# Causal depthwise filters of a two-layer decoder: from four 128x32 column tiles to sixteen 32x32 tiles, with a new order of all steps

## What is computed

```python
v_direct = silu(causal_conv4(h @ Wv))               # 128 channels = 4 heads x 32
delta_out = delta_rule_chunkwise(q, k, v_direct, beta)      # chunks of 32: a triangular solve in each
paths = [fir(v_direct, w) for w in (fir_w3, fir_w7, fir_w15, fir_w31)] + [delta_out]
# fir: causal, depthwise: y[ch, t] = sum_j w[ch, j] * v[ch, t - j]
mix = softmax(router(h, *paths) / tau)              # per token, head and path
o = sum(mix_i * path_i) * (1 - p) + v_direct * p    # then a norm per head, Wo, residual, layer norm
```

## Time and profile before

| | us |
|---|---|
| median of 3 runs (lowest, highest) | 1003.74 (1002.26, 1004.86) |
| span of the profiled execution | 1004.1 |
| PE busy | 932.3 |
| DVE busy | 742.6 |
| ACT busy | 650.3 |
| POOL busy | 334.5 |

### The profile page before, as it was taken

One profiled execution on the slowest core, in us unless ns is written; L12 is line 12 of the kernel. 1 busy time (PEld: TensorE's weight loads), 2 busy tenths in 40 slices (PEclk: granted clock), 3 DMA queues, 4 the chain that ended last, 5 costly groups with the idle time before them and its releaser, 6 DMA issues.

```text
span 1004.1 us, 22014 instructions
## 1 busy us (share of the span) xinstructions
PE 932.3 (93%) x7958; PEld 593.9 (59%) x7958; DVE 742.6 (74%) x2882; ACT 650.3 (65%) x1474; POOL 334.5 (33%) x720
## 2 busy tenths in 40 slices
PE   6988899999986989999999999999977899999996
...
DVE  3556789899899986866374797869999996665514
...
PEclk7999999999987799999999999999986999999998
...
GB/s 308 175 2 1 1 1 52 2 83 14 95 128 75 43 70 17 44 22 12 1 12 1 11 11 1 53 60 94 90 97 76 57 21 22 2 11 1 12 1 32
DMA packets 77692, 45.44 MB, mean 45 GB/s; under 512 B 53008, under 2 KB 68880, under 8 KB 77328
## 3 DMA queue, kind: packets, MB, share of 16 engines
...
## 4 chain that ended last, share of the span: by engine, by line
PE 57%; DVE 27%; ACT 8%; POOL 4%; issue 3%; DMA 0%; SPq 0%; POOLq 0%; ACTq 0%; DVEq 0%
PE psum L1101 7%; DVE pool L1588 5%; DVE sol_t L1593 5%; PE psum L558 5%; PE psum L1091 4%; PE psum L859 4%; PE psum L833 3%; PE psum L831 3%; PE psum L994 3%; DVE pool L1531 3%; PE psum L920 3%; PE psum L1085 2%; PE psum L1087 2%; ACT pool L1823 2%; PE psum L567 2%
## 5 line engine op out<-in xcount | busy, mean ns | idle before, releaser
L1809 ACT ACTIVATE pool<-psum 128x512 f32<-128x512 f32 x144 | 84.0, 595 | 64.4 <-PE psum L558 22.4
L2185 POOL TENSOR_SCALAR small<-small 128x4 f32<-128x4 f32 x88 | 22.2, 252 | 283.6 <-DVE small L1173 281.4
L1823 ACT ACTIVATE pool<-pool,small 128x128 f32<-128x128 f32 x224 | 91.5, 486 | 27.3 <-POOL small L2190 27.1
L558 PE MATMUL psum<-sb_const,pool 128*128 128x128 f32 x672 | 100.9, 283 | 6.4 <-ACT pool L1823 2.9
L920 PE MATMUL psum<-pool,firw 128*32 128x512 f32 (+7 forms) x960 | 103.2, 571 | 0.0
L558 PEld LDWEIGHTS psum<-sb_const,pool 128*128 128x128 f32 x672 | 79.3, 145 | 37.9 <-issue 22.3
L2188 POOL TENSOR_TENSOR small<-small,minus_half 128x4 f32<-128x4 f32 x88 | 92.2, 1048 | 7.3
L994 PE MATMUL psum<-pool,sb_l1a 128*128 128x512 f32 x192 | 88.6, 612 | 0.0
L1101 PEld LDWEIGHTS psum<-sb_l1f,pool 128*128 128x128 f32 x640 | 77.2, 192 | 11.3 <-issue 9.5
L1101 PE MATMUL psum<-sb_l1f,pool 128*128 128x128 f32 x640 | 82.8, 278 | 0.0
L1404 DVE TENSOR_TENSOR pool<-pool,psum 128x512 f32<-128x512 f32 x80 | 52.4, 682 | 37.8 <-ACT pool L2095 16.2
...
## 6 DMA issues: line engine op xcount, KB each, us to landing
...
```

Source lines behind the costliest of these rows:

```text
L558: m = e.transpose(f.ap[:, part(b)], src[:, part(b)], ident)
L1809: e.activation(slot(g, i), f.ap, ACT.Copy).then_inc(f.emptied, 1)
L1823: m = e.activation(dst[:, part(b)], src[:, part(b)], ACT.Identity, bias=v["nm"][:, b:b + 1], scale=v["r"][:, b:b + 1])
```

## The change

What it does, part by part:
- **b_fir** is one step with four banks. The contraction of 32 rows is now 4 shifts x 8 channels, and the 32 outputs of a tile are 4 filters x 8 channels. Row tile r is a head, column tile c a quarter of its channels. All filters are padded with zeros to eight tap groups: 8 x 16 = 128 products a group of 32x32, bank r for row tile r.
- **b_sh** writes v to DRAM in four DMAs, which reorder the channels so that a read of stride 4 finds shift s on partitions s, s+4, ...; the four reads go to partitions of stride 4.
- **b_ez** is one multiply on POOL of the first three columns of each of 16 blocks by a column of zeros and ones; it also waits for `s_b2`.
- **b_mx, b_ac, b_w, b_lt**: paths now lie as (head, batch, quarter, filter, channel), so the mixing weights are laid out by head and spread first (`spread`), and the sum over filters is taken inside the tile: low and high halves (POOL for slots 3 and 4, DVE for 5 and 6), then neighbours.
- **Setup**: `s_w` (new) sorts the taps on PE in 16 small products and copies them; `s_b2` clears `firw` and fills it in 16 small multiplies. `l1a` is loaded by 18 DMAs instead of one, since the router's rows for slots 3 to 6 are reordered.
- **ORDER** is new as a whole.

```diff
+NKG = 8
-    firw, itau = sb("firw", [P, nfg * 4, CH]), sb("inverse_tau", [P, NH])
+    firw, itau = sb("firw", [P, NKG, 4, 32]), sb("inverse_tau", [P, NH])
-for _name in ("b_kk", "b_at"):
+for _name in ("b_kk", "b_at", "b_fir"):
...
 def b_sh(g, k):
+            by_row = kept.rearrange("(r u c) m -> r c u m", r=4, c=4)
-            e.dma_start(kept, slot(g, 5)).then_inc(sem(f"v_out{a}"), 16)
-            o.wait_ge(sem(f"v_out{a}"), 16 * (g // NA + 1))
+            for r in range(4):
+                e.dma_start(by_row[r], slot(g, 5)[32 * r:32 * r + 32]).then_inc(sem(f"v_out{a}"), 16)
+            o.wait_ge(sem(f"v_out{a}"), 64 * (g // NA + 1))
             for s in range(4):
-                e.dma_start(vsh[32 * s:32 * s + 32, :, s:],
-                            kept.rearrange("(c p) m -> p c m", c=4)[:, :, 0:GT - s]).then_inc(sem(f"shifted{a}"), 16)
+                e.dma_start(vsh[s:P:4, :, s:],
+                            kept.rearrange("(u c) m -> u c m", c=4)[:, :, 0:GT - s]).then_inc(sem(f"shifted{a}"), 16)
...
-        for p_ in ("l1a", "l0f"):
-            load(p_)
+        load("l1a", 0, rw1 + 256)
+        load("l1a", rw1 + 5 * 256)
+        for c in range(4):
+            for f in range(4):
...
+                e.dma_start(dst[32 * c + 8 * f:32 * c + 8 * f + 8], src).then_inc(sem("ld_l1a"), 16)
+        load("l0f")
...
 def b_fir(g, k):      # PE
-            f = begin("b_fir", g, "s", k)
+            heads_f = [begin("b_fir", g, f"h{r}") for r in range(4)]
...
+            for kg in range(NKG):
+                for r in range(4):
+                    r_ = slice(32 * r, 32 * r + 32)
+                    for c in range(4):
+                        m = e.matmul(b4(heads_f[r].ap)[32 * c:32 * c + 32, :, 4 * kg:], firw[r_, kg, c, :],
+                                     vsh[r_, c, :, 0:P - 4 * kg], start=kg == 0, stop=kg == NKG - 1)
+                    if kg == NKG - 1:
+                        m.then_inc(heads_f[r].filled, 1)
...
 def b_mx(g, k):       # DVE
-            e.tensor_tensor(hd(p), hd(f.ap), rep(w3[:, :, k], DH), ALU.mult).then_inc(f.emptied, 1)
-            if k >= 2:
+            e.tensor_tensor(slot(g, 3 + k).rearrange("p (q f u) -> p q f u", f=4, u=8),
+                            f.ap.rearrange("p (q f u) -> p q f u", f=4, u=8), share, ALU.mult).then_inc(f.emptied, 1)
+            if k == 3:
...
+                e.tensor_tensor(low, low, high, ALU.add).then_inc(*o.link())
...
 def b_fir(g, k):      # ACT
-            evacuate("b_fir", g, 3 + k, k)
+            for r in range(4):
+                f = full("b_fir", g, f"h{r}")
+                e.activation(slot(g, 3 + r), f.ap, ACT.Copy).then_inc(f.emptied, 1)
...
 def b_ez(g, k):       # POOL
-            for s in range(1, 4):
-                settle()
-                e.memset(vsh[32 * s:32 * s + 32, :, :, 0:s], 0.0).then_inc(*mark("edge_zeroed", 3 * g + s))
+            o.wait_ge(made, MADE["s_b2"])
...
+            e.tensor_tensor(cells, cells, shift_col[:, 0:3].unsqueeze(1).to_broadcast([P, NP, 3]), ALU.mult).then_inc(
+                *mark("edge_zeroed", g + 1))
```

More of the change, by code:

```diff
@@ L48 @@
[L48 to L82, removed]
@@ L103 @@
-b_x.32-41/4 b_vT/5 b_x.42-44/4 b_fir.1/5 b_q2/6 f_na/7 b_fir.2-3/5 b_kk/5 b_fir.0/6 b_x.45-52/4 b_ag/5 b_x.53-58/4
-b_vT/6 b_x.59/4 b_ss/6 b_x.60-61/4 b_xo/4 b_tr/7 b_q/7 b_k/7 b_qs/7 b_v/7 b_vs/7 b_sol/5 b_x.0-1/5 b_qn/6 b_x.2-3/5
-b_gg/6 b_x.4-6/5 b_ks/7 b_k2/7 b_fir.1/6 b_x.7/5 b_fir.2/6 b_x.8-20/5 b_fir.3/6 b_rs/4 b_xt/4 b_x.21/5 b_rl/4 b_u.0/4
-b_x.22/5 b_sh/7 b_kk/6 b_x.23-26/5 b_ag/6 b_x.27-31/5 b_p.0/4 b_q2/7 b_ss/7 b_x.32-34/5 b_u.1/4 b_x.35-39/5 b_ez/7
-b_x.40-43/5 b_qn/7 b_x.44-47/5 b_gg/7 b_x.48-51/5 b_fir.0/7 b_vT/7 b_p.1/4 b_x.52-53/5 b_fir.1/7 b_sol/6 b_x.0/6
@@ new lines @@
+b_ez/2 b_x.61/0 b_x.8-9/1 b_tr/3 b_qn/2 b_x.10/1 b_xo/0 b_gg/2 b_rs/0 b_x.11-14/1 b_v/3 b_xt/0 b_k/3 b_x.15-16/1 b_q/3
+b_x.17-18/1 b_vs/3 b_ks/3 b_x.19/1 b_k2/3 b_rl/0 b_x.20-24/1 b_qs/3 b_fir/2 b_x.25-26/1 b_sh/3 b_x.27-31/1 b_q2/3 b_ez/3
+b_kk/2 b_x.32/1 b_u.0/0 b_x.33-38/1 b_ag/2 b_ss/3 b_x.39/1 b_qn/3 b_x.40-41/1 b_p.0/0 b_x.42-48/1 b_vT/3 b_sol/2
+b_x.49/1 b_u.1/0 b_x.50-51/1 b_gg/3 b_x.52-54/1 b_x.0/2 b_x.55/1 b_x.1-4/2 b_fir/3 b_x.5/2 b_x.56/1 b_x.6-7/2 b_x.57/1
+b_x.8/2 b_x.58/1 b_x.9/2 b_x.59/1 b_x.10/2 b_x.60/1 b_x.11-12/2 b_x.61/1 b_x.13-14/2 b_xo/1 b_x.15-22/2 b_rs/1
```

263 lines of the change are left out of this document (174 added, 89 removed).

## The result

| | before | after |
|---|---|---|
| median of the runs shown | 1004.22 us | 1010.33 us (1008.83 to 1012.08) |
| ratio, 95% interval | | 1.0059 (1.004 to 1.0079) |
| span of the profiled execution | 1004.1 us | 1007.0 us |
| mean granted clock of TensorE | 0.959 | 0.955 |
| filter line: PE busy | 103.2 us | 69.3 us |

The account below looks back on a forecast made before the run. Bound by PE, with two patches bound by DVE. Shortening the two stretches with filters gave -38 us, banks +3, other terms zero: -35 from the profiled 1004.1 us, so 969 us; range 947 to 998.

Parts of the forecast that it names:

- until DVE is as dense as in its densest stage: In 100 to 400 and 560 to 850 us, with filters: both stretches shorten until DVE is 92% busy throughout.
- the 18 and 20 us of the sum: Forecast shortening of the two stretches with filters: 18 us from 100 to 400 us, 20 us from 560 to 850.
- -38: Forecast saving in us over both stretches with filters together, before 3 us were added for banks.
- My own sign: Whole kernel: the forecast is wrong if PE's idle time grows from 72 towards 110 us.
- Rival 2: DVE keeps the end: only line 920's 24.9 us on the chain halve, to 12.5; 992 us; includes lossy order; chance 0.15.
- instead of 6.4: Forecast length in us of one new filter step on PE, with sixteen tiles running at once.
- instead of 50: Forecast saving in us of PE time by the new filters over all eight groups.
- rival 1: Fewer filter tiles at once: four, about 1095 us (chance 0.08); eight, 1003 (0.04); ten or twelve, 985 (0.10).
- the forecast 3 us: Cost in all of filter steps holding four PSUM banks at once, put between nothing and 4.8 us.
- 747 forecast: DVE's busy time over the whole kernel after the change, in us.
- Hidden: Setup's 5 us more DVE work, in the first 100 us, costs zero; 5 us if group 0's b_q, b_k, b_v wait.
- I had zero: Extra b_sh transfers delay work behind on SP by 1.7 us a group, covered by other work; 13 us without cover.

## Why the prediction was wrong

- **Bound.** The step that failed is "until DVE is as dense as in its densest stage", the 18 and 20 us of the sum. I read PE's busy share of 91 and 94% in the two stretches as a bound and asked how short they could be if DVE reached 92% all over them. But DVE already was at 91 and 92% in the solving stages, where six of the eight filter steps stand; the slack of my average lay elsewhere, and no run shows work from elsewhere coming over because PE has room. The stages went from 125 and 98 to 124 and 105 us. The cut of 23.6 us in the kernel before, worth nothing, shows that this part of the "-38" was not to be had by shortening alone. My own sign, PE's idle time growing from 72 towards 110 us, came half true: 93.5.
- **Groups 0 and 4.** Outside the solving stages, too, the saving did not arrive: the wait for four banks (3.29 us) and the lower clock behind it (0.73 over the step) ate it at group 0 (b_kk 0.55 us later than with the old filters there). The sum had no term for the clock.
- **The chain.** Rival 2 took line 920's 24.9 us on the chain for time that shortens with it. It does not either: at group 0 the filter was on the chain with another wait 1.4 us behind it.
- **Filters on PE.** Direction right, size off: 7.95 us at full clock (1.00, five of eight steps; 9.4 to 10.5 in the three that met the lower clock, 0.73 to 0.82 over the step) instead of 6.4, 33.9 us saved instead of 50. So 25.3/7.95: 3.2 times the four-tile rate, 12.7 of sixteen tiles. This was rival 1 in a mild form: the pauses of the loads fit a limit of 64 unfinished instructions (they end 31 or 32 ns after the record 65 ahead, above), and four instructions times sixteen tiles reach it. That sixteen tiles would last what the 64-record step with its four lasts was my estimate; they took 1.24 times as long (7.95 instead of 6.4).
- **Banks.** The wait is near the forecast 3 us: the filter line now waits 5.0 us (3.29 and 1.74), all for DVE's convolution by the profile, where it waited for nothing before. What I missed is that it falls on groups 0 and 4 alone and that the clock is lower behind it (0.73 and 0.82 over these two steps).
- **DVE.** Its work stayed what it was, as forecast: 738.0 us after, 744.7 with the new steps in the old order, 747 forecast.
- **Setup and start.** "Hidden" held in the new order (the changed kernel is 0.7 us ahead of the old steps there at 100 us) and failed in the old one, 5 us. There DVE is 53% busy, and the loss still stays.
- **Queue and POOL.** Right for the filters: no wait of theirs for the shifted rows or the cleared edges is shown. For what stands behind on SP I had zero, and there b_ag's and b_sol's transfers have come onto the chain, 9 and 19 us of it; what they cost was not tested.
- **Order.** I gave the search credit for passing time on and set a lossy order inside rival 2. With old steps the new order is 20 us slower, all of it in the two solving stages (125 and 98 to 129 and 114 us). Why is open.
- **Rivals.** None on the slow side had this mechanism. The missing one was a wait uncovered right behind the filter (seen at groups 0, 1 and 4), and, in the changed kernel, right before it.
